# Message stage of a graph kernel: TensorE multiplies zeros into the accumulator ahead of each step's weights

## The reference

```
h = silu(edge_lengths_embedding @ fc_w1 / sqrt(8))            # 82500 x 64
w = (h @ fc_w2 / sqrt(64)).reshape(-1, 5, 64)                 # five weights for each edge and feature
s, v = node_features of the sender                            # 64 scalars, 64 vectors
dot, crs = v . sh1, v x sh1                                   # sh1: the edge's unit vector times sqrt(3)
m0 = (w0 * s + w3 * dot / sqrt(3)) / sqrt(2)
m1 = (w1 * s * sh1 + w2 * v + w4 * crs / sqrt(2)) / sqrt(3)
agg = segment_sum([m0, m1], receiver) / 16
```

## Time and profile before

| | us |
|---|---|
| median of 3 runs | 2991.58 |
| profiled execution, whole | 2960.97 |
| its span | 2959.3 |
| message stage, 163 steps from L652 to L652 | 1277.8 |

### The profile page before, as it was taken

The page is one execution under the profiler, slowest core; times in us unless marked ns, Lnnn a source line. Parts: engine busy times, 40 slices in busy tenths (PEclk is TensorE's granted clock), DMA queues, the critical chain, the costliest instruction groups (busy, mean ns, idle before and its releaser), DMA issues. The chain is left out here.

```text
span 2959.3 us, 42276 instructions
## 1 busy us (share of the span) xinstructions
PE 1920.9 (65%) x9895; PEld 1281.3 (43%) x9895; DVE 2147.3 (73%) x3429; ACT 1533.4 (52%) x4251; POOL 1634.1 (55%) x1807
## 2 busy tenths in 40 slices
PE   3666666666777756665994367666666676666675
PEld 2343433333444433333441245555455554455554
DVE  6676876667888866663554588788787887888884
ACT  6576775665777766661332244444434444444353
POOL 4555655555666655553221666666666666666652
PEclk7888887887888888876997688788777787887788
DMA  5222222222222222235886666666666666666651
GB/s 188 64 72 69 74 73 62 63 65 59 79 80 78 81 64 64 67 116 107 230 229 186 177 173 174 170 174 170 171 172 166 174 172 169 175 177 166 176 160 42
DMA packets 157415, 379.09 MB, mean 128 GB/s; under 512 B 47810, under 2 KB 63298, under 8 KB 157186
## 3 DMA queue, kind: packets, MB, share of 16 engines
q0 software_dynamic: 100544, 309.00, 37.5%
q1 hardware_dynamic: 44946, 68.53, 8.1%
q10 hardware_dynamic: 11904, 1.34, 0.4%
HBM read 353.36 MB, written 37.07 MB: 132 GB/s over the span
## 5 line engine op out<-in xcount | busy, mean ns | idle before, releaser
L1369 POOL DMA_INDIRECT kv_e<-kv_rows,edge x752 | 716.7, 953 | 414.3 <-issue 217.2
L507 POOL DMA_INDIRECT feat<-in_x_rows,idx x664 | 696.1, 1048 | 223.1 <-issue 219.2
L543 ACT ACTIVATE vsh<-feat,rec_a 128x256 f32<-128x256 f32 x1980 | 806.7, 497 | 7.3 <-remote 4.0
L1552 PE MATMUL ps_sum<-kv_e,ident 128*128 128x264 f32 x1504 | 473.4, 477 | 361.8 <-issue 253.2
L573 PE MATMUL ps_w<-w,hid 64*128 64x320 f32 x1320 | 306.3, 596 | 384.2 <-DVE msg L652 377.2
L1552 PEld LDWEIGHTS ps_sum<-kv_e,ident 128*128 128x128 f32 x1504 | 352.8, 240 | 466.9 <-issue 271.4
L593 PE MATMUL ps_a<-msg,hot 128*64 128x257 f32 (+2 forms) x3936 | 491.2, 387 | 55.7 <-issue 55.2
L593 PEld LDWEIGHTS ps_a<-msg,hot 128*64 128x64 f32 x3936 | 292.4, 146 | 281.8 <-issue 188.8
L573 PEld LDWEIGHTS ps_w<-w,hid 64*128 64x128 f32 x1320 | 150.5, 243 | 482.5 <-issue 456.0
L106 DVE SCALAR_TENSOR_TENSOR hot<-count,origin,rec 128x256 f32<-128x256 f32 x164 | 78.6, 479 | 285.3 <-remote 218.0
L529 ACT ACTIVATE hid<-ps_h 128x256 f32<-128x256 f32 x165 | 61.7, 374 | 423.1 <-PE ps_h L564 287.4
(11 more groups left out here) (417 smaller groups left out, 2892.2 us busy)
## 6 DMA issues: line engine op xcount, KB each, us to landing
ef<-in_ef_t SPq DMA_DIRECT2D x84, 256.0 KB
kv_e<-kv_rows,edge POOLq DMA_INDIRECT x752
rows_e<-rows SPq DMA_DIRECT2D x41, 272.0 KB, 2.8
feat<-in_x_rows,idx POOLq DMA_INDIRECT x664
rows_e<-in_ef_t SPq DMA_DIRECT2D x1, 7446.0 KB, 26.9
kv_rows<-kv SPq DMA_DIRECT2D x20, 260.0 KB, 2.5
rows_e<-in_ef_t SPq DMA_DIRECT2D x1, 3706.0 KB
x<-x_rows SPq DMA_DIRECT2D x23, 128.0 KB
```

What stands on the lines that cost most here:

```text
L507: pool.indirect_dma_start(out=feat[:, c, u, :, :].rearrange("p a b -> p (a b)"), out_offset=None, in_=g.x_rows, in_offset=bass.IndirectOff ...
L543: ins = act.activation(vsh[:, u % 2, c, j, :, :], feat[:, c, u % TURN, :, :], ACT.Copy, scale=rec_a[:, u % 2, c, 1 + j:2 + j])
L1369: pool.indirect_dma_start(out=kv[:, u, s, :], out_offset=None, in_=g.kv_rows, in_offset=bass.IndirectOffsetOnAxis(ap=edge[:, u, s, DH + 1: ...
L1552: mm = pe.matmul(out, g.ident[:], kv[:, u, s, D:], start=(s == 0), stop=False, skip_group_check=True)
```

## The change

`w2` loses its second dimension: each half of the rows holds `fc_w2` once. A tile `blank` of 128x128 zeros is new, cleared by VectorE ahead of the loop. In each step TensorE first waits until VectorE has added the sums that stand in this step's bank, and then multiplies `blank` twice by 512 columns of `count512` (the numbers 0 to 511) into the whole bank, the first time with `start=True`. Then come the old wait and the old work; its sums now all accumulate (`start=False`) onto the zeros.

```diff
-                    sp.dma_start(g.w2[half * NH:(half + 1) * NH, half, place * MUL:(place + 1) * MUL],
+                    sp.dma_start(g.w2[half * NH:(half + 1) * NH, place * MUL:(place + 1) * MUL],
...
-                cols = g.w2[:, :, path * MUL:(path + 1) * MUL]
+                cols = g.w2[:, path * MUL:(path + 1) * MUL]
...
+        blank = sb("blank_m", [P, P])
...
-                    mm = pe.matmul(ps_w[:, c, 0:NPATH * MUL], hid[rows, u % 2, at:at + P], g.w2[rows, half, :],
+                    mm = pe.matmul(ps_w[:, c, 0:NPATH * MUL], hid[rows, u % 2, at:at + P], g.w2[rows, :],
...
-            pe.wait_ge(m_clear, 2)
+            pe.wait_ge(m_clear, 3)
             with pe.Fori(0, turns) as t:
                 for u in range(TURN):
                     i = t * TURN + u
 
+                    pe.wait_ge(m_acc, i + 2)
+                    for n in range(2):
+                        pe.matmul(ps_a[:, u % 2, :], blank[:], g.count512[:], start=(n == 0), stop=False,
+                                  skip_group_check=True)
                     pe.wait_ge(m_prod, i + 1 + TURN)
                     weights(i + 1, u + 1)
...
-                            first, last = c == 0 and part == 0, c == CHUNKS - 2 and part == 2
+                            last = c == CHUNKS - 2 and part == 2
...
-                                mm = pe.matmul(out, hot[:, u % 2, c + side, :], msg[:, u % 2, c + side, lo:hi], start=first,
+                                mm = pe.matmul(out, hot[:, u % 2, c + side, :], msg[:, u % 2, c + side, lo:hi], start=False,
...
+            dve.memset(blank[:], 0.0).then_inc(m_clear, 1)
-            dve.wait_ge(m_clear, 2)
+            dve.wait_ge(m_clear, 3)
...
-                g.w2 = sb("w2", [2 * NH, 2, NPATH * MUL], within=edges)
+                g.w2 = sb("w2", [2 * NH, NPATH * MUL], within=edges)
```

## The result

The change took 3035.8 us (median of 20 runs, 2997.84 to 3059.86), the kernel before beside it 3020.97 us (20 runs, 2950.02 to 3064.38). The ratio is 1.0183, 95% interval 1.013 to 1.0235: slower by 1.8%, just under the 2% of the forecast's classes. A ratio leaves out executions over 1.5% above the fastest of their kernel, as disturbed by a slower state of the chip; here that keeps 5 of the 20 before and 16 of the 20 after. Over all forty the medians differ by 0.5% and the means (3015.8 and 3034.0 us) by 0.6%. So the change is slower by 0.5 to 1.8% according to how one counts. The profiled execution took 3037.37 us, span 3035.7. Forecast: 3100, range 2850 to 3215, "slower by over 2%" at 0.57. The direction was right and the size too large: between the two profiled executions it is +76.4 us where my sum said +108, and between the medians only +15.

The account below looks back on a forecast made before the run. Bound: the message stage's chain through TensorE, ScalarE and VectorE, with late completions beside GpSimd's gathers. 81.5 pairs x 17.0 = 1386 instead of 1278 us, +108 on 2961 gives 3069, 3100 on the median's scale; range 2850 to 3215.

Parts of the forecast that it names:

- Zeros, hidden work: TensorE, message stage: zeros take 2.0 us a step warm, 4.0 cold, nearly all in idle time; nothing if hidden.
- The waits, start=False: TensorE's new wait for m_acc ends before the old one would; same number of sums accumulate; both cost 0.
- w2: Table stage, ahead of the loop: memset, scaling and space of w2 halve, one small memset is added; taken as 0.
- Clock: Even steps' weights on TensorE run warm, 1.46 instead of 2.50 us; alone worth 1.05 us a pair, 86 us in all.
- L658 of k+1 comes earlier, the pause shrinks, the completion is late: Quick pairs: L658 (old L652) 5.5 us behind the last, GpSimd's pause 0.74 us, sums' completion only behind its second group.
- The cycle: Message stage repeats pairs of 13.6, 18.3, 19.4 and 16.8 us, 17.0 us a pair: 1386 instead of 1278 us, +108.
- the pattern of rows 7: Pair behind a long one: GpSimd's first gather takes 2.28 us, no pause, one-hots wait 7.78 us, weights cold again.
- The starting point: Message stage of the profiled execution before: 1277.8 us, 42 quick pairs; execution of 2961 us, 1% added for the median.
- rival B: No change: clock still falls before L652, or stalls alternate with pairs of 12, 15.6 us each; 2990 us, chance 0.20.
- Rival A: Faster: clock stays up, completions come in time, 12.8 us a pair, -235 us, 2756 us; chance 0.18 in full.
- Its deciding point: Rival A holds if the even step's m_used comes before GpSimd's second group of gathers gets going.
- Rival C: TensorE binds: cold zeros of 4.0 us make 18.0 us a pair, +190, 3180 us; counted within the forecast's 0.57.

Follow-up runs that it names:

- e7: The kernel before with only the halved w2, no zeros and no wait for m_acc: 3029.01 us beside 2987.84 for the kernel before.
- e5: The change itself, timed again in another session: 2447.94 us beside 2534.05 for the kernel before, ratio 0.9669.
- e2: The kernel before, without zeros, with GpSimd waiting for m_used before copying its next gather indices: 2547.59 us, ratio 1.0014 to the kernel before.
- e10: The changed kernel with zeros in even steps only and GpSimd waiting for m_used: 2774.84 us, one run, beside 2987.84 for the kernel before.
- e11: Zeros in even steps only and GpSimd's wait for m_used, timed in another session: 2779.42 us beside 3232.13 for the kernel before, ratio 0.8701.
- e12: The changed kernel with the message stage's gathers replaced by SyncE's plain transfers of fixed rows: 2682.2 us, one run, beside 3232.13 for the kernel before.

## Why the prediction was right, and where not

*Zeros, hidden work: right.* 1.35 us weights, and L650 waits 49.0 us in all in the whole stage where it waited 43.9, 0.06 us a pair more (7.0 of it by name for the weights' product, before 24.6; the rest mostly "remote"). A record took 545 ns (355.0/652), between my 0.49 and its double.

*The waits, start=False: as said.* L587 waits 2.8 us in all for `sums`. *w2:* taken as 0, neither shown nor refuted (e7).

*Clock: right in direction, in size partly by luck.* I priced warm even weights at 1.05 us a pair, 86 us in all; e5 against e2 gives 0.99 and 80.3. But in e2 the even weights were cold only in part, 1.93 us in the mean. Its fully cold pairs (2.50 us) take 13.62 us and its warm ones 12.03, so a cold pair gains 1.6 us: my price was too low, and fewer pairs than I thought were there to gain it. The Trainium skill ("TensorE: Matmul & The Clock Gate", Part 1, "What's actually happening") says that activity releases the throttled clock. Here, in time, the stage's clock rose from 0.89 (e2) to 1.00 (e5), and the pair did get shorter.

*"L658 of k+1 comes earlier, the pause shrinks, the completion is late": that late completions go with GpSimd's gathers is now more than an inference.* e10 and e11 put the pause back and the idle time fell to 128 and 139 us; e12 took GpSimd's gathers away and it fell to 0. That the zeros bring more of these stalls is seen in single pairs of the profile after, but not shown for the kernel's time, since e7 had as many without them. And the rule has a condition that the trace of before could not show: on another level the same 0.74 us pause costs nothing (e5).

*The cycle: mis-sized, and this is the step that failed.* I took 13.6, 18.3, 19.4, 16.8, mean 17.0 us a pair, because I let the pair behind a stall start cold ("the pattern of rows 7"). The zeros at the stall's end run ahead of them: after a stall the weights took 1.35 us, and the even step's sums, whose records end at 420.86 us, were signalled at once (one-hots at 421.94), though GpSimd had been issuing since 417.40. Why these came through and those of the next step did not, no run shows. So 12.0 came in the place of 19.4, and the next pair took 18.7. Cycle of the rows above: 18.4, 12.0, 18.7, 17.4, mean 16.6; stage mean 2 x 8.205 = 16.4. With 16.4 in place of 17.0 the sum gives 81.5 x 16.4 = 1337, +59 instead of +108. The other 16 us of the profiles' difference arise behind the stage, in untouched code. Both parts are of the size by which runs of one kernel differ: the kernel before alone spreads over 114 us here.

*The starting point was a quick execution.* My +108 was added to a stage of 1277.8 us with 42 quick pairs, and I took that mix for the kernel's own. Only 1% was added for the median, while the median of twenty is 3021 us, 60 us above the profile, and the stage took 1378.5 us in an execution of e7, which has no zeros either. The cycle of 17.0 us a pair is nearly what that execution did (16.9). That the direction came out right by 0.5 to 1.8% is in part luck. The chance I gave to rival B ("stalls alternate with pairs of 12", 15.6 a pair, 0.20) was too low: that mixture is what happened, only with more stalls. B's class, a difference within 2%, is what was measured.

*Rival A (faster) was wrong here and right elsewhere.* In the session of e5 it is what the change does: -3.3%. I had estimated 12.8 us a pair, from 13.0 of TensorE's own work; it was 11.96. TensorE, zeros included, was busy 973.4 of 974.3 us there, so its own work comes to 12.0 and not 13.0. But that isn't what sets the pace: with zeros in the even steps alone e10's quickest pairs took 11.97 too, and e2's, without zeros, 12.03. What is left is the chain through ScalarE and VectorE, whose one wait in e5 is the 66.0 us for ScalarE's `vsh`. Its deciding point, `m_used` ahead of GpSimd's second group, was the right one: in e5 the one-hots, which need it, start at 406.01, the group at 406.98. That the level and not the zeros brings this about, it could not say. *Rival C* did not set the stage: a record of the zeros is busy for 545 ns, not 1 us.

**Open:** what sets the level (one chip number occurs at both); by what path GpSimd's gathers hold TensorE back; how much of the 0.5 to 1.8% on a late level is due to the zeros, to `w2` or to neither; what the zeros are worth on a late level once GpSimd waits (the wait alone was timed in time only, 1.0014).

## What to carry to other kernels

When an engine waits for a completion whose work the trace shows long done, look at what other engines were issuing at that moment, and try to move that, before speeding up the chain: warm weights saved 1 us a pair, and beside waits of 7 us that saving did not show in the time. A wait that lets GpSimd start its gathers only when TensorE's signal is through cost nothing where completions came in time (1.0014) and where they did not it took 261 us off the kernel with zeros in even steps (3036 to 2775 us); both together were 13% faster than the kernel before (0.8701). And time the kernel before beside every variant, and profile more than one execution of it: this change was 3.3% faster in one session and 0.5 to 1.8% slower in another.

## What the runs showed of the hardware that was not expected

- One kernel, one core, five sessions: 2534, 2544, 2988, 3021, 3232 us, each with a spread of under 4%. With GpSimd waiting, much of that is gone: e10 and e11 took 2775 and 2779 us where the kernel before took 2988 and 3232. Behind the message stage, in code that no run changed, every profile in time took 1416 to 1422 us and every profile on a late level 1628 to 1652.
- TensorE's matmuls themselves come apart while GpSimd issues gathers: single records some 0.7 us apart, and 106.8 us of idle time in front of them over the stage of the change, where e5 has none (its row is shown above) and e10, whose GpSimd waits, has none either.
```profile
L598 PE MATMUL ps_a<-msg,hot 128*64 128x257 f32 (+2 forms) x3912 | 518.2, 388 | 106.8 <-issue 105.4
```
- Some first gathers of a group took 2.28 us, most others 0.95 to 1.01. The prediction put that down to a long rest of GpSimd, and that is wrong: e5 has 16 of them in its first 260 us, each behind a pause of 0.74 us, and the gather behind its longest rest (28 us) took 1.01. What makes them slow stays open. One of e5's:
```profile
78.62 2.28 POOL L508 DMA_INDIRECT feat<-in_x_rows,idx  x1 [0.46 <-issue]
```
